# A graph network on one core: sum products ahead of query products, four index slots, node passes in four stages

## The chip, the cores and the metric

The kernel runs on one core of a Trainium2 chip. The metric is the device time of one execution in microseconds (us); lower is better. The engines of the core are TensorE (PE; its weight loads are listed as PEld), VectorE (DVE), ScalarE (ACT), GpSimd (POOL) and SyncE (SP), which issues most of the plain DMAs. Each engine runs its own stream of instructions in order, and the engines wait for each other on counting semaphores.

## The reference

Two graph layers over 6250 nodes with 128 features and 100,000 edges, sorted by destination. All data are float32.

```
x = norm(x + L0(x))          # attention layer
x = norm(x + L1(x))          # message layer

L0: q, k, v = X@Wq, X@Wk, X@Wv                     # 8 heads of 16
    scores  = sum(q[dst] * k[src]) / 4             # per edge and head
    alpha   = softmax of the scores over the edges of each dst
    agg     = segment_sum(alpha * v[src], dst)
    h1      = layer_norm(X + agg@W0)
    return layer_norm(h1 + relu(h1@fc1 + b)@fc2 + b)

L1: for the first and for the second half of the edges, with its own W1, W2:
        m = [x[src], edge_attr, req] ; h = relu(m@W1 + b1)@W2 + b2
        h_sum[dst] += h
    return relu(((1 + eps)*x + h_sum)@Wu + bu)
```

## The kernel before

After a short preparation (tables of chunks, key/value/query rows written to DRAM as kvq_tab) the kernel has three stages.

**First loop.** Edges are taken in chunks of 14 x 128 = 1792; there are 56. A chunk's edges end in a window of 128 nodes. GpSimd gathers the key and value rows of the edges' sources with one indirect DMA per 128 edges (L657), 14 a chunk, in four pieces of 4, 3, 4 and 3, into a ring of four chunk slots. TensorE spreads the window's queries over the edges (`queries`, L1050: 14 products of 128 x 128, each in two halves, so 28 instructions; four pieces). VectorE multiplies by the keys and reduces to scores, keeps the running maxima along the sorted edges by scans (`across`, L1404 to L1406, with help of TensorE's end transposes L1064/L1065 and carried transposes L1074/L1075), builds the one-hot masks (L1435) and weights the values (L1440) with the exponentials of ScalarE (L841 to L843). TensorE sums them into the window (L1090, 14 products, 28 instructions). A pass of the loop works on several chunks at once: the queries of the next chunk, the maxima of the last (`a_`), the sums of the one before (`b_`), the averages of the one before that (`c_`, L1080/L1081). In a pass TensorE's order is: end transposes, query pieces 0 and 1, carried transposes, averages' transpose, sums, query pieces 2 and 3.

The gathers are held by semaphores: piece 0 waits for the weighted values of the chunk four back (l_pvb), piece 1 for its sums (l_agg), piece 2 for the queries of the chunk one back (l_q), piece 3 for the end transposes of the chunk two back (l_lr).

**Node passes.** The 50 tiles of 125 nodes are taken in 10 groups of 5. A pass works on three groups: `new` (agg@W0, L1132, residual and first norm), `mid` (transposes, hidden layer L1115, relu L868, second product L1142) and `old` (second and third norm, transposes, then the products with W1 of both directions, L1152, copied by ScalarE, L906, and stored to y_tab by SyncE, L474). VectorE begins `old` at L1514. `passes3` writes two opening passes, a loop of 8 and two closing passes.

**Second loop.** 56 chunks again. GpSimd gathers rows of y_tab (L710), 14 DMAs a chunk, into a ring of four slots (yg). TensorE puts the attributes' share of the hidden layer into PSUM (L1187), VectorE adds it to the gathered rows (`hidden_rows`, L1575, semaphore m_hid), ScalarE takes the relu (L940), TensorE sums over the edges (L1200, semaphore m_agg), and finished windows go through Wu, the last norm and out. The indices (idx1), destination columns (dcol1) and attributes (eat) of a chunk are loaded by SyncE into two slots each. SyncE loads the attributes of chunk p+3 when the transposed attributes have been copied (m_eT), and the indices of chunk p+2 when VectorE has taken chunk p (m_hid). GpSimd's `gather_edges` waits for the indices (m_ix) and for the sums of the chunk four back (m_agg), and ahead of its second and third piece for the attribute transposes (m_eTp) and products (m_u).

Both loops are unrolled by four (`passes4`); every engine's counters advance by registers.

## Time and profile before

| | |
|---|---|
| median of 3 runs | 2862.45 us (2857.86 to 2866.96) |
| the profiled execution | 2882.01 us, span 2880.1 us |
| TensorE busy | 1588.5 us (55%), mean granted clock 0.711 |
| GpSimd busy | 1566.9 us (54%) |
| VectorE busy | 1430.9 us (50%) |
| ScalarE busy | 746.1 us (26%) |

The shares are averages over three stages. In a timeline row the number in brackets is the engine's idle time before the instruction and what ended it; "issue" means that it waited for nothing that the profile shows. In a row of windows each engine has its busy time and, behind x, the number of its instructions that began in the window; then come the granted TensorE clock (1.00 is 2.4 GHz, 0.50 is 1.2 GHz), the share of time in which the DMA engines were busy, and GB/s.

### The profile page before, as it was taken

The page shows a single profiled execution, that of the slowest core. Times are in us where ns is not written, and L with a number is a line of the kernel's source. Part 1 is how long each engine was busy: PE and PEld are TensorE (multiplying, and loading weights), DVE is VectorE, ACT ScalarE, POOL GpSimd, SP SyncE. Part 2 cuts the span into 40 slices and gives each one's busy share as a digit, 9 for nine tenths or more (in the row PEclk, how much of TensorE's full clock was granted, in tenths as well). Part 3 has the DMA queues.
Part 4 walks back from the last instruction along what each step waited for, and adds up shares of the span by engine and source line. Part 5 has one row for each costly group of instructions (what it writes and reads, how often), then busy time and mean ns, then how long its engine had stood idle before and what let it go on. Part 6 is the DMA issues. An engine that isn't in the chain of part 4 may idle for free.

```text
span 2880.1 us, 32266 instructions
## 1 busy us (share of the span) xinstructions
PE 1588.5 (55%) x7344; PEld 1255.8 (44%) x7345; DVE 1430.9 (50%) x2992; ACT 746.1 (26%) x1502; POOL 1566.9 (54%) x1648
## 2 busy tenths in 40 slices
PE   5315556565556565555777345555555555555546
PEld 3215555555555555554555233333433333333424
DVE  3226666666666666666555234343443333344435
ACT  2213333333333333333454111111111111111111
POOL 3346666666666666663111455655666665556653
PEclk8557676767776777776998667766676666666667
DMA  5474444444444444441000112211221121112211
GB/s 167 138 200 127 143 131 141 131 138 133 129 142 131 141 131 138 133 128 60 18 27 27 56 42 51 52 49 48 54 51 51 50 52 50 47 48 51 53 49 38
DMA packets 148162, 255.22 MB, mean 89 GB/s; under 512 B 73948, under 2 KB 99088, under 8 KB 147996
## 3 DMA queue, kind: packets, MB, share of 16 engines
q0 software_dynamic: 65072, 160.39, 19.9%
q1 hardware_dynamic: 81186, 92.67, 10.1%
q10 hardware_dynamic: 1870, 1.78, 0.2%
q8 instruction: 12, 0.20, 0.0%
q14 instruction: 22, 0.18, 0.0%
HBM read 233.05 MB, written 28.04 MB: 91 GB/s over the span
## 4 chain that ended last, share of the span: by engine, by line
issue 33%; PE 22%; DVE 16%; another core or an unknown queue 13%; DVEq 5%; DMA 5%; ACT 4%; SPq 1%; POOL 0%; ACTq 0%; POOLq 0%
PE ps L1090 8%; PE ps L1050 6%; DVE arena L1566 3%; DVE arena L1435 2%; DVE arena L1575 2%; PE ps L1200 2%; DVEq L1595 2%; PE ps L1187 1%; ACT arena L873 1%; PE ps L1152 1%; DVEq L1594 1%; DVE arena L1440 1%; DMA first<-d 1%; DVEq L1592 1%
## 5 line engine op out<-in xcount | busy, mean ns | idle before, releaser
L710 POOL DMA_INDIRECT arena<-y_tab,arena x784 | 741.9, 946 | 512.6 <-issue 494.1
L657 POOL DMA_INDIRECT arena<-kvq_tab,arena x784 | 749.0, 955 | 471.3 <-issue 240.6
L1050 PE MATMUL ps<-arena 128*128 128x128 f32 x1596 | 325.7, 363 | 331.0 <-issue 251.4
L1200 PEld LDWEIGHTS ps<-arena 128*128 128x128 f32 x1568 | 285.5, 247 | 413.2 <-issue 394.1
L1200 PE MATMUL ps<-arena 128*128 128x128 f32 x1568 | 308.0, 336 | 282.8 <-issue 273.5
L1050 PEld LDWEIGHTS ps<-arena 128*128 128x128 f32 x1596 | 299.5, 275 | 349.9 <-issue 345.5
L1090 PE MATMUL ps<-arena 128*128 128x136 f32 x1568 | 319.2, 391 | 173.3 <-DVE arena L1440 88.5
L1090 PEld LDWEIGHTS ps<-arena 128*128 128x128 f32 x1568 | 309.5, 295 | 190.6 <-issue 190.6
L940 ACT ACTIVATE arena<-arena 128x512 f32<-128x512 f32 x224 | 118.9, 567 | 1029.7 <-DVE arena L1575 662.7
L1575 DVE TENSOR_TENSOR arena<-ps,arena 128x512 f32<-128x512 f32 x224 | 127.8, 616 | 511.2 <-remote 299.1
L1187 PE MATMUL ps<-w1blk,eaT 113*128 x456 | 271.3, 677 | 59.4 <-issue 55.6
L809 ACT ACTIVATE arena<-arena 128x1792 f32<-128x1792 f32 x58 | 191.5, 3301 | 0.0
L1568 DVE TENSOR_REDUCE arena<-arena 128x128 f32<-128x1792 f32 x57 | 182.4, 3200 | 2.0
L1404 DVE COPY arena<-arena 8x1 f32<-8x1 f32 x56 | 7.9, 141 | 337.5 <-ACT arena L843 337.5
L832 ACT ACTIVATE arena<-ps 128x136 f32<-128x136 f32 x56 | 16.0, 285 | 507.4 <-remote 476.9
L1388 DVE TENSOR_REDUCE arena<-arena 128x32 f32<-128x512 f32 x224 | 139.2, 621 | 8.4 <-issue 0.5
L1386 DVE TENSOR_TENSOR arena<-ps,arena 128x512 f32<-128x512 f32 x224 | 135.9, 607 | 5.7 <-remote 3.0
L1187 PEld LDWEIGHTS ps<-w1blk,eaT 113*128 113x128 f32 x456 | 90.9, 240 | 75.1 <-issue 74.9
L1566 DVE TENSOR_TENSOR arena<-ps,arena 128x1792 f32<-128x1792 f32 x57 | 114.3, 2006 | 4.8 <-ACT arena L930 4.8
L1440 DVE TENSOR_TENSOR arena<-arena,ps 128x896 f32<-128x896 f32 x112 | 115.6, 1068 | 0.0
L1435 DVE TENSOR_TENSOR arena<-ps,arena 128x1792 f32<-128x1792 f32 x56 | 112.3, 2005 | 0.0
L1601 DVE TENSOR_TENSOR arena<-arena,ps 128x128 f32 x56 | 16.2, 288 | 190.2 <-issue 179.7
(243 smaller groups left out, 1980.5 us busy)
## 6 DMA issues: line engine op xcount, KB each, us to landing
arena<-d SPq DMA_DIRECT2D x58, 897.0 KB
arena<-kvq_tab,arena POOLq DMA_INDIRECT x784
arena<-y_tab,arena POOLq DMA_INDIRECT x784
eat<-ea SPq DMA_DIRECT2D x59, 112.0 KB
ea<-in_edge_attr_dram SPq DMA_DIRECT2D x2, 3125.0 KB, 20.0
y_tab<-arena SPq DMA_DIRECT2D x10, 625.0 KB
kvq_tab<-arena SPq DMA_DIRECT2D x6, 937.5 KB
arena<-kvq_tab SPq DMA_DIRECT2D x59, 64.0 KB
```

The lines of the kernel that those rows point to most:

```text
L657: g.indirect_dma_start(kv_s[:, r, t, :], None, kvq_tab.rearrange("n (a d) -> (n a) d", a=3), bass.IndirectOffsetOnAxis(ap=v3(idx, RING)[:, ...
L710: g.indirect_dma_start(yg_s[:, r, t, :], None, y_tab, bass.IndirectOffsetOnAxis(ap=v3(idx1, 2)[:, u, t:t + 1], axis=0)).then_inc(m_g[r][k] ...
L809: a.activation(hotT.rearrange("n (u g e) -> n u g e", u=2, g=G)[:, u, :, :], line.rearrange("n (e g) -> n g e", g=G), ACT.Relu, scale=-1.0 ...
L1050: last = mm(bank(k)[:, t * D:(t + 1) * D], hotT_s[:, u, s0 + t, :], v3(qwin, 2)[:, u, :])
L1090: last = mm(sums, hot_s[:, u, t, :], contrib_s[:, u, t * RW:(t + 1) * RW], start=(t == 0), stop=(t == G - 1))
L1187: mm(bank(j)[:, 0:n * D], eaT_s[:, u, k * P:(k + 1) * P], w1blk[:, ds(way + a0 * D, n * D)]).then_inc(m_u, 1)
L1200: last = mm(bank(6 + u)[:, 0:W], yg_s[:, r, t, :], hot1_s[:, u, t, :], start=(t == 0), stop=(t == G - 1))
L1435: tt(hot_s[:, u, :, :], columns[:, None, :].to_broadcast([P, G, P]), dcr_s[:, u, :, None].to_broadcast([P, G, P]), ALU.is_equal).then_inc( ...
L1440: tt(contrib_s[:, u, s0:s1, :, 0:DH], kv_s[:, r, s0:s1, D:2 * D].rearrange("p g (h w) -> p g h w", h=H), weights.rearrange("p (g h) -> p g ...
L1566: link(tt(hot1_s[:, u, :, :], columns1[:, None, :].to_broadcast([P, G, W]), dcr1[:, :, None].to_broadcast([P, G, W]), ALU.is_equal))
L1568: v.tensor_reduce(v3(hsum, 2)[:, u, :], hot1_s[:, u, :, :].rearrange("p g n -> p n g"), AX_X, ALU.add).then_inc(m_hot, 1)
L1575: tt(rows_, v3(bank(j)[:, 0:n * D], n), rows_, ALU.add).then_inc(m_hid, 1)
```

## The change

Three things are changed.

- First loop: in TensorE's pass the sum products (L1090) are placed ahead of the query pieces 0 and 1, the carried transposes and the averages' transpose. No other engine's order changes.
- Second loop: idx1, dcol1 and eat have four slots. SyncE loads all three for chunk p+4 in one place, after m_hid of chunk p; the first four chunks are loaded ahead of the node passes. GpSimd no longer waits for m_eTp and m_u. The attribute transposes still run three chunks ahead.
- Node passes: the last part of `old`, the products with W1 and their copy, becomes a fourth stage `out_` one pass later. These products go to banks 1 to 3, right behind the transposes of `mid`, and ScalarE copies them in two instructions ahead of the relus. ScalarE takes the square root of the second norm ahead of the relus, that of the third behind them, and finishes the third norm ahead of the first norm's root. VectorE computes the scales of the third norm ahead of the new group. TensorE puts the transposes of the third norm's result between the third and the fourth tile of the second hidden product. There are three opening passes, a loop of 7 and three closing passes. GpSimd's clearing of the accumulators moves behind the first group's sum.

```diff
@@ -221,8 +220,9 @@
         hsum = carve(2 * W)
         sel = carve(4)
-        idx1 = carve(2 * G).bitcast(I32)
-        dcol1 = carve(2 * G)
+        idx1 = carve(RING * G).bitcast(I32)
+        dcol1 = carve(RING * G)
+        eat = carve(RING * G * EA)
         dcr1 = carve(G)
         outT = carve(W)
...
@@ -467,6 +469,19 @@
             sp.wait_ge(l_qw[1], all_e)
             sp.sem_inc(l_over, 1)
+            sp.wait_ge(l_over, 4)
+            sp.wait_ge(s_eac, 32)
+            sp.wait_ge(s_tabi[1], 48)
+            eat_s = v3(eat, RING)
+
+            def load_chunk(chunk, r):
+                off = sp.value_load(tab_sb[1][0:1, ds(5 * chunk, 1)], min_val=0, max_val=NB * CH)
+                sp.dma_start(eat_s[:, r, :], ea1[ds(off, CH), :].rearrange("(p g) f -> p (g f)", g=G)).then_inc(m_at[r], 16)
+                sp.dma_start(v3(idx1, RING)[:, r, :], i1[ds(off, CH)].rearrange("(p g) -> p g", g=G)).then_inc(m_ix[r], 16)
+                sp.dma_start(v3(dcol1, RING)[:, r, :], d1[ds(off, CH)].rearrange("(p g) -> p g", g=G)).then_inc(m_ld[r], 16)
+
+            for c in range(RING):
+                load_chunk(c, c)
 
             sp.sem_inc(n_yfree, 2)
...
@@ -482,41 +497,19 @@
...
             def sp_msgs(r, new, a_, b_, c_):
                 u = r % 2
                 if new is not None:
-                    next_attr(new + 3, 1 - u)
                     sp.wait_ge(s_eac, 32)
                     sp.wait_ge(m_hid, spent)
-                    sp.wait_ge(m_dcr, prepared)
-                    load_edges(new + 2, u)
+                    load_chunk(new + RING, r)
                     sp.reg_add(spent, spent, NP_)
-                    sp.reg_add(prepared, prepared, 1)
+                    if r == RING - 1:
+                        sp.reg_add(loaded, loaded, 16)
                 if c_ is not None:
                     base = sp.value_load(tab_sb[1][0:1, ds(5 * c_ + 1, 1)], min_val=0, max_val=N - W)
...
@@ -691,41 +684,28 @@
 
             def gather_edges(r):
-                u = r % 2
                 pool.wait_ge(m_buf, 4)
-                pool.wait_ge(m_ix[u], landed)
+                pool.wait_ge(m_ix[r], landed)
                 pool.wait_ge(m_agg, slot_free)
                 for k, (s0, n) in enumerate(PIECES):
-                    if k in (1, 2):
-                        pool.wait_ge(m_buf, 4)
-                        pool.wait_ge(*((m_eTp, turned_) if k == 1 else (m_u, asked)))
                     for t in range(s0, s0 + n):
                         g.indirect_dma_start(yg_s[:, r, t, :], None, y_tab,
-                                             bass.IndirectOffsetOnAxis(ap=v3(idx1, 2)[:, u, t:t + 1], axis=0)).then_inc(m_g[r][k], 16)
+                                             bass.IndirectOffsetOnAxis(ap=v3(idx1, RING)[:, r, t:t + 1], axis=0)).then_inc(m_g[r][k], 16)
                 pool.reg_add(slot_free, slot_free, 1)
-                pool.reg_add(asked, asked, NP_)
-                pool.reg_add(turned_, turned_, 1)
 
             def gather_ring():
                 for r in range(RING):
-                    if r == 2:
-                        pool.reg_add(landed, landed, 16)
                     gather_edges(r)
                 pool.reg_add(landed, landed, 16)
...
             with pool.Fori(0, n1):
                 gather_ring()
-            pool.wait_ge(m_buf, 4)
-            pool.wait_ge(m_ix[0], landed)
-            pool.wait_ge(m_ix[1], landed)
             g.memset(mark[:, 1:2], 0.0)
 
...
@@ -873,37 +853,35 @@
                 return last
 
-            def act_pass(new, mid, old):
+            def act_pass(new, mid, old, out_):
                 if new is not None:
                     a.activation(v3(nTa, GRP), by_tile(new), ACT.Copy).then_inc(n_aT, 1)
...
                     act.wait_ge(n_hTp, mid + 1)
                     a.activation(nTh, bank(0, 2)[:, 0:GRP * P], ACT.Copy).then_inc(n_hT, 1)
-                    relu(mid, 0)
                 if old is not None:
                     sqrt(1, old, norm2)
+                if out_ is not None:
+                    act.wait_ge(n_y, out_ + 1)
+                    act.wait_ge(n_yfree, out_ + 1)
+                    y_ = yst[:, ds((out_ % 2) * (GRP * 2 * D), GRP * 2 * D)]
+                    a.activation(y_[:, 0:(GRP - 1) * 2 * D], bank(2, 2)[:, 0:(GRP - 1) * 2 * D], ACT.Copy)
+                    a.activation(y_[:, (GRP - 1) * 2 * D:GRP * 2 * D], bank(1)[:, D:3 * D], ACT.Copy).then_inc(n_ys, 1)
                 if mid is not None:
-                    relu(mid, 1)
-                if mid is not None:
-                    relu(mid, 2)
-                    relu(mid, 3)
+                    for c in range(FC):
+                        relu(mid, c)
                 if old is not None:
                     sqrt(2, old, norm2)
-                if new is not None:
-                    sqrt(0, new, norm1)
-                if old is not None:
                     act.wait_ge(n_r[1], old + 1)
                     normalised(v3(res2, GRP), v3(res2, GRP), norm2).then_inc(n_x1, 1)
                 if new is not None:
+                    sqrt(0, new, norm1)
                     act.wait_ge(n_r[0], new + 1)
                     normalised(v3(res, GRP), v3(res, GRP), norm1).then_inc(n_n1, 1)
...
                     act.wait_ge(n_x1c, old + 1)
                     a.activation(nTx, bank(0, 2)[:, 0:GRP * P], ACT.Copy).then_inc(n_xT, 1)
-                    act.wait_ge(n_y, old + 1)
-                    act.wait_ge(n_yfree, old + 1)
-                    a.activation(yst[:, ds((old % 2) * (GRP * 2 * D), GRP * 2 * D)], bank(4, 3)[:, 0:GRP * 2 * D], ACT.Copy).then_inc(n_ys, 1)
 
             act.sem_inc(n_ys, 1)
...
@@ -1063,6 +1039,16 @@
                     tp(left_right[0:H, 0:P], ends[:, :, G - 1], ident[:, :])
                     tp(left_right[0:H, P:2 * P], ends[:, :, 0], ident[:, :]).then_inc(l_lr, 1)
+                if b_ is not None:
+                    pe.wait_ge(l_hot, minus2)
+                    if c_ is not None:
+                        pe.wait_ge(l_cur, minus3)
+                    pe.wait_ge(l_pva, minus2)
+                    for t in range(G):
+                        if t == PVA:
+                            pe.wait_ge(l_pvb, minus2)
+                        last = mm(sums, hot_s[:, u, t, :], contrib_s[:, u, t * RW:(t + 1) * RW], start=(t == 0), stop=(t == G - 1))
+                    last.then_inc(l_agg, 1)
                 if new is not None:
                     queries(w, 0, True)
...
@@ -1115,42 +1091,56 @@
                 last.then_inc(n_f1, 1)
 
-            def pe_pass(new, mid, old):
+            def rows_y(t):
+                return bank(2, 2)[:, t * 2 * D:(t + 1) * 2 * D] if t < GRP - 1 else bank(1)[:, D:3 * D]
+
+            def pe_pass(new, mid, old, out_):
                 if mid is not None:
                     pe.wait_ge(n_h1, mid + 1)
+                    if out_ is not None:
+                        pe.wait_ge(n_xT, out_ + 1)
                     transposes(h1, n_hTp)
+                if old is not None:
+                    pe.wait_ge(n_z, old + 1)
+                if out_ is not None:
+                    pe.wait_ge(n_xT, out_ + 1)
+                    for t in range(GRP):
+                        if t == GRP - 1 and mid is not None:
+                            pe.wait_ge(n_hT, mid + 1)
+                        last = mm(rows_y(t), nTx[:, t * P:(t + 1) * P], w1x[:, :])
+                    last.then_inc(n_y, 1)
+                if mid is not None:
                     pe.wait_ge(n_hT, mid + 1)
-                    pe.wait_ge(n_ys, 1 if old is None else old + 1)
                     hidden(mid, 0)
                     hidden(mid, 1)
-                if mid is not None:
-                    pe.wait_ge(n_f1s, mid * FC + 1)
-                    hidden(mid, 2)
+                if out_ is not None:
+                    pe.wait_ge(n_ys, out_ + 2)
                 if new is not None:
                     pe.wait_ge(n_aT, new + 1)
...
                     last.then_inc(n_emb, 1)
                 if mid is not None:
-                    pe.wait_ge(n_f1s, mid * FC + 2)
-                    hidden(mid, 3)
-                    pe.wait_ge(n_f1s, mid * FC + FC)
-                    if old is not None:
-                        pe.wait_ge(n_v[1], old + 1)
+                    for c in range(2, FC):
+                        pe.wait_ge(n_f1s, mid * FC + (c - 1))
+                        hidden(mid, c)
                     for t in range(GRP):
+                        if t == GRP - 2 and old is not None:
+                            turn_rows(new, old)
                         for c in range(FC):
+                            if t == 0:
+                                pe.wait_ge(n_f1s, mid * FC + (c + 1))
                             last = mm(bank(2, 2)[:, t * D:(t + 1) * D], v3(ffT, FC)[:, c, t * P:(t + 1) * P], fc2_sb[:, c, :],
                                       start=(c == 0), stop=(c == FC - 1))
                     last.then_inc(n_f2, 1)
-                if old is not None:
-                    if new is not None:
-                        pe.wait_ge(n_v[0], new + 1)
-                    pe.wait_ge(n_x1, old + 1)
-                    transposes(res2, n_xTp)
-                    pe.wait_ge(n_xT, old + 1)
-                    for t in range(GRP):
-                        last = mm(bank(4, 3)[:, t * 2 * D:(t + 1) * 2 * D], nTx[:, t * P:(t + 1) * P], w1x[:, :])
-                    last.then_inc(n_y, 1)
+                elif old is not None:
+                    turn_rows(new, old)
+
+            def turn_rows(new, old):
+                if new is not None:
+                    pe.wait_ge(n_v[0], new + 1)
+                pe.wait_ge(n_x1, old + 1)
+                transposes(res2, n_xTp)
 
             pe.sem_inc(n_xTp, 1)
...
@@ -1511,7 +1500,8 @@
                     dve.wait_ge(n_xTp, old + 1)
                     hc3 = v3(h1c[:, ds((old % 2) * (GRP * D), GRP * D)], GRP)
-                    link(tt(q3, hc3, v3(bank(2, 2)[:, 0:GRP * D], GRP), ALU.add))
+                    tt(q3, hc3, v3(bank(2, 2)[:, 0:GRP * D], GRP), ALU.add).then_inc(n_z, 1)
+                    dve.wait_ge(n_z, old + 1)
                     statistics(q3, n_v[1], norm2)
                     dve.wait_ge(n_s[1], old + 1)
...
@@ -1519,15 +1509,13 @@
                     link(tt(q3, q3, xg(old), ALU.add))
                     statistics(q3, n_v[2], norm2)
+                    dve.wait_ge(n_s[2], old + 1)
+                    scales(norm2, n_r[1])
                 if new is not None:
 
...
                     link(tt(r3, xg(new), v3(bank(0, 2)[:, 0:GRP * D], GRP), ALU.add))
                     statistics(r3, n_v[0], norm1)
-                if old is not None:
-                    dve.wait_ge(n_s[2], old + 1)
-                    scales(norm2, n_r[1])
-                if new is not None:
                     dve.wait_ge(n_s[0], new + 1)
                     scales(norm1, n_r[0])
```

Left out of it: GpSimd's clearing of the accumulators, SyncE's three removed load functions for the second loop, the wider semaphore lists and counters, the passes with a fourth argument in `passes3`, the indices of slots in ScalarE's and TensorE's second loop, and the sums' old place (the ten lines shown as added after the end transposes are removed behind the averages' transpose).

## Rows read from the trace of the kernel before

**Rows 1.** Windows, all engines, by stage; columns: window, length, busy us (instructions) per engine, granted clock, DMA.
```profile
119.00:1355.00 1236.00, 702.58 (x3558) 638.61 (x3558) 768.42 (x1681) 425.76 (x733) 744.14 (x779) 0.71 0.45 136
1355.00:1607.00 252.00, 167.09 (x862) 125.23 (x862) 124.23 (x471) 118.17 (x213) 44.51 (x22) 0.85 0.07 26
1614.00:2880.00 1266.00, 667.88 (x2756) 461.49 (x2756) 506.17 (x730) 173.99 (x510) 742.04 (x785) 0.68 0.19 49
```

**Rows 2.** Timeline of a pass of the first loop: start, length, engine, line, operation, count [idle before, releaser].
```profile
623.87 0.95 POOL L657 DMA_INDIRECT arena<-kvq_tab,arena  x1 [3.69 <-remote]
...
624.90 2.66 PE L1050 MATMUL ps<-arena 128*128 128x128 f32 x14
...
625.95 0.14 DVE L1404 COPY arena<-arena 8x1 f32<-8x1 f32 x1 [6.66 <-ACT arena L843]
...
628.57 0.39 PE L1081 MATMUL ps<-arena 128*1 128x136 f32 x2
...
631.98 5.98 PE L1090 MATMUL ps<-arena 128*128 128x136 f32 x28 [3.02 <-DVE arena L1440]
...
637.79 0.67 PE L1050 MATMUL ps<-arena 128*128 128x128 f32 x4
...
641.66 0.69 SPq L365 DMA_DIRECT2D arena<-i  x1
...
643.82 2.06 PE L1050 MATMUL ps<-arena 128*128 128x128 f32 x8 [0.36 <-issue]
...
644.89 0.96 POOL L657 DMA_INDIRECT arena<-kvq_tab,arena  x1 [3.73 <-remote]
...
647.41 0.94 POOL L657 DMA_INDIRECT arena<-kvq_tab,arena  x1 [0.30 <-issue]
```

**Rows 3.** Windows of the same pass, before and during the gap at L1050.
```profile
623.87:638.50 14.63, 11.04 (x57) 10.02 (x56) 12.02 (x26) 7.21 (x12) 11.27 (x12) 0.66 0.54 164
638.50:643.80 5.30, 0.64 (x2) 0.47 (x2) 1.69 (x5) 0.00 (x0) 2.05 (x3) 0.69 0.29 82
```

**Rows 4.** Windows of the second loop, over one run of gathers.
```profile
2078.40:2089.10 10.70, 10.70 (x49) 7.43 (x49) 8.08 (x12) 2.78 (x9) 8.21 (x9) 0.72 0.27 66
2089.10:2117.00 27.90, 3.83 (x13) 2.04 (x12) 1.27 (x3) 1.44 (x4) 18.30 (x20) 0.60 0.21 54
```

**Rows 5.** Timeline of GpSimd (POOL) and SyncE (SP) in the second loop, restarts of the gathers.
```profile
1677.69 0.94 POOL L710 DMA_INDIRECT arena<-y_tab,arena  x1 [11.20 <-issue]
...
2056.17 0.95 POOL L710 DMA_INDIRECT arena<-y_tab,arena  x1 [9.09 <-issue]
...
2076.14 0.35 SPq L501 DMA_DIRECT2D arena<-i  x1
...
2078.45 0.95 POOL L710 DMA_INDIRECT arena<-y_tab,arena  x1 [5.06 <-issue]
...
2122.32 0.95 POOL L710 DMA_INDIRECT arena<-y_tab,arena  x1 [9.12 <-issue]
```

**Rows 6.** Timeline of a node pass.
```profile
1492.46 2.42 PE L1152 MATMUL ps<-w1x,arena 128*128 128x256 f32 x10 [1.68 <-ACT arena L903]
...
1493.47 0.82 DVE L1514 TENSOR_TENSOR arena<-arena,ps 128x640 f32<-128x640 f32 x1
...
1495.07 1.24 ACT L906 ACTIVATE arena<-ps 128x1280 f32 x1 [2.66 <-PE ps L1152]
...
1500.69 0.19 DVE L1492 RECIPROCAL arena<-arena 128x5 f32<-128x5 f32 x1 [4.67 <-ACT arena L864]
...
1514.93 0.82 DVE L1514 TENSOR_TENSOR arena<-arena,ps 128x640 f32<-128x640 f32 x1
```

**Rows 7.** Timeline of the start of the second loop.
```profile
1607.44 0.20 ACT L913 ACTIVATE mark<-eps_ln 128x1 f32<-128x1 f32 x1 [7.14 <-DMA y_tab<-arena]
...
1611.82 0.36 SPq L501 DMA_DIRECT2D arena<-i  x1
...
1614.21 0.99 POOL L710 DMA_INDIRECT arena<-y_tab,arena  x1 [18.46 <-DMA arena<-i]
```

More of the change, by code:

```diff
@@ L535, in _ @@
             sp.wait_ge(f_dma, stored)
+            for r in range(RING):
+                sp.wait_ge(s_eac, 32)
+                sp.wait_ge(m_at[r], loaded)
+                sp.wait_ge(m_ix[r], loaded)
+                sp.wait_ge(m_ld[r], loaded)
         @block.gpsimd
@@ L672, in _, with pool_pass @@
             pool.wait_ge(s_w4, 16 * (12 + 2 * (EG - 1)))
[L673 to L677 removed]
+            def pool_pass(new, mid, old, out_):
                 if new is not None:
@@ L1081, in pe_edges @@
                     mm(turned[0:1, W:W + RW], uc[:, w:w + 1], cur_s[:, w, :]).then_inc(l_ra, 1)
-                if b_ is not None:
-                    pe.wait_ge(l_hot, minus2)
-                    if c_ is not None:
-                        pe.wait_ge(l_cur, minus3)
-                    pe.wait_ge(l_pva, minus2)
-                    for t in range(G):
-                        if t == PVA:
-                            pe.wait_ge(l_pvb, minus2)
-                        last = mm(sums, hot_s[:, u, t, :], contrib_s[:, u, t * RW:(t + 1) * RW], start=(t == 0), stop=(t == G - 1))
-                    last.then_inc(l_agg, 1)
                 if new is not None:
@@ L1504, in _, with dve_pass @@
             rowb = lambda k: rows[:, k:k + 1, :].to_broadcast([P, GRP, D])
-            def dve_pass(new, mid, old):
+            def dve_pass(new, mid, old, out_):
                 xg = lambda at: v3(xs[:, ds(at * (GRP * D), GRP * D)], GRP)
```

84 lines of the change are left out of this document (29 added, 55 removed).

## The prediction

> **What bounds the kernel now.** I read the stages first, by windows. The first loop (the node features' attention, 56 chunks of 1792 edges) takes about 1236 us, the node passes 252 us, the second loop (the messages, 56 chunks again) 1266 us [rows 1]. In no stage is an engine busy all the time; GpSimd comes nearest in both loops, with one gather instruction of 0.95 us for 128 rows and 0.30 us between two [rows 2]. That is 14 x 1.25 = 17.5 us a chunk, 980 us for 56, against 21.0 us a chunk in the first loop (GpSimd starts again after its long wait at 623.87 and at 644.89, [rows 2]) and about 22.1 in the second (from the restart at 2056.17 to that at 2122.32 lie 66.2 us and three chunks, [rows 5]). So the question in both loops is what GpSimd and TensorE wait for beyond 17.5 us.
>
> The order of time in one pass of the first loop shows it [rows 2]. The 28 halves of the sum products run from 631.98 to 637.96. Four halves of the next chunk's third query product follow, and then TensorE nearly stands still: the next eight in a row begin only at 643.82. The window over that gap counts 2 matmuls in 5.30 us, against 57 in the 14.63 us before it [rows 3]. SyncE crawls in the same stretch (an index load takes 0.69 us to issue). GpSimd, whose next piece waits for the sums (l_agg), goes on only at 644.89, after 3.73 us of waiting. VectorE waits 6.66 us in such a pass (L1404), for the exponentials (L843), which wait for the end transposes (L1064) behind the queries in TensorE's order.
>
> The second loop shows the same thing more plainly. GpSimd starts a run of gathers at 2078.4, after a pause. For 10.7 us TensorE works normally: 49 matmuls. In the next 27.9 us it starts 13, while GpSimd issues 20 gathers; it recovers only when GpSimd has stopped [rows 4]. The pauses between runs are 5.06 and 9.12 us [rows 5]. I read this as one behaviour: after a stretch of uninterrupted gathers TensorE (and SyncE) get almost no instructions through, until GpSimd pauses and about 2.5 us have passed. In the first loop the stretch ends some 110 to 120 TensorE instructions after GpSimd's restart (57 matmuls and 56 weight loads in [rows 3]); in the second 49 and 49 plus its register instructions. GpSimd's pauses are then not only a loss: they are what lets TensorE move. The Trainium skill says otherwise: in "Runtime: NRT & Kernel Launch", "Instruction fetch mechanics", an engine's instruction buffer refills itself in the background and its cost is mostly hidden. By that page a run of gathers would cost TensorE nothing; the rows above show 13 matmuls in 27.9 us, and the rows decide.
>
> **Part 1, the sum products ahead of the queries.** Nothing is added or removed; the 28 halves of L1090 move ahead of the first two query products, the carried transposes and the averages' transpose. Those now stand between sums and the end transposes, which release VectorE's half of the pass. Before, they ran while VectorE worked on the masks, so they cost nothing. The cost from rows: 14 query halves 2.66 us, and about 1.2 us for the small products behind them (an estimate, three times the 0.39 us of L1081's pair), 3.9 us in all [rows 2]. Without any standstill the old cycle is sums 6.0, the third and fourth query products 1.6 to 3.0 (14 halves at 0.12 to 0.21 us), end transposes and exponentials about 1.5 (the last 1.05 lie between 624.90 and 625.95) and VectorE's part from L1404 to the start of the sums 6.0: 15.1 to 16.5 us. The new one is 19.0 to 20.4, above GpSimd's 17.5. Now the standstill. The old 21.0 is that cycle with 5.3 us of it. In the new order the sums begin about 12 to 14 us after the restart of GpSimd instead of 8 (from 623.87 to 631.98), so the standstill, which began 14.6 us after the restart, catches them half done; l_agg, for which GpSimd's next chunk waits, then comes after it. On the other side GpSimd's third piece waits for the queries (L653), now later than the sums, and may pause there 2 to 3 us while TensorE is working, which would spare part of the standstill. If the pause spares all of it, the pass takes 20.2 us (17.5 + 2.7): 0.8 us less than now. If it spares nothing, it takes up to 24.9 (21.0 + 3.9). A pass in between, one standstill for each restart at the queries, comes to about 22.3. I take that, as the chain really is longer: +1.3 us a chunk, 56 x 1.3 = **+73 us**, bounds -45 and +218.
>
> **Part 2, four slots for the indices.** It removes three kinds of wait of GpSimd: for the index load, for the attribute transposes (m_eTp) and for the attribute products (m_u); and one of SyncE's two stops a pass. Now a chunk's indices are loaded only when VectorE has taken the chunk two before (m_hid), by a SyncE that itself crawls. The restart at 2078.45 comes 2.3 us after such a load was issued, at 2076.14 [rows 5]. With four slots GpSimd is held only by m_agg of the chunk four back. The instructions saved (two loads of registers a pass) are on no path. If GpSimd were the bound, the loop would fall to 17.5 us a chunk: 4.6 x 56 = 258 us less. But the rows say that TensorE moves in the pauses. With the deeper slots GpSimd first runs 5 chunks in a row (88 us; now the first run, from 1614.21 on [rows 7], ends 52 us later, 11.20 us ahead of 1677.69 [rows 5]). Then it restarts when a sum is done. If TensorE finishes the next chunk (49 halves, 11 to 13 us at the rate of the first window of [rows 4]) before that run of 17.5 is over, the run doubles to 35 us and TensorE stands still for 24: a cycle of 47 to 49 us for two chunks, 24 a chunk, +106 us. If the standstill catches it just before the end of the sums, GpSimd pauses after each chunk, as in the first loop, 20.7 a chunk, -78 us. Today's runs of 28 and of 14 gathers alternate: 44 + 22 us for 3 chunks. I take no difference in the steady part, **0 us**, with those bounds.
>
> The loads before the node passes do gain a little. Now GpSimd starts at 1614.21, 6.8 us after the last store of the node passes has landed (1607.44), because the index load is issued at 1611.82 [rows 7]. With the indices in place it can start about 1608.5: **-6 us**.
>
> **Part 3, node passes in four stages.** A full pass takes 21.46 us (L1514 at 1493.47 and 1514.93) [rows 6]. The message products of a group (L1152, 2.42 us) and their copy (L906, 1.24 us) lie in its cycle between the norm and the next group's copies; they go a pass later, beside VectorE. VectorE's 4.67 us of waiting for a square root behind a relu (L1492) goes as well, since the root is put ahead. In exchange the second root waits behind all four relus, and the products stand ahead of the first hidden product. Adding up VectorE's own instructions with the three roots and one norm that it waits for gives 18.4 us, 3 less. That is 8 passes x 3.0 = **-24 us**; the pass more at the ends holds only the last product and copy, which the old last pass had too. Bounds: 8 x 4.67 = -37, and 0 if the new order only moves the wait. The memsets of GpSimd (L673, L674) move behind the first group's sum; they overlap TensorE and VectorE in both kernels.
>
> **The sum.** Against the profiled execution's own 2882.0 us (span 2880.1): +73 + 0 - 6 - 24 = +43, 2925. The median of the three runs shown, 2862.45, is 0.7% below it, so I forecast 2862 + 43 = **2905 us**.
>
> **Rivals.** (a) The standstill in the first loop stays where it is: the pause at the queries lets TensorE through, the pass remains at 21.0, and in the second loop GpSimd pauses after every chunk at 20.7. Then 0 - 78 - 30 = -108: 2754 us. For it: the old first loop does just that, at 21.0, every pass. Against it: the sums end nearer to the standstill by the 3.9 us moved ahead of them in time. It decides when the sums of a pass end within 14 us of GpSimd's restart. This is the one on the other side. (b) Only the node passes and the start count, the two loops keep their cycles: -30, 2832 us. The change of the loops would then do nothing; the near-equality of cycle and run length (17.3 us of gathers and 3.7 of pause in each pass) speaks for it. (c) Both loops lose: +73 or more, and the second loop in double runs at 24, +106, less 30: about 3010 us. (d) GpSimd really is the bound and both loops go to 17.5: 2862 - 196 - 258 - 30 = 2380; by the page on instruction fetch this would be the outcome for the second loop alone, 2862 - 258 - 30 = 2574. The windows of the second loop [rows 4] speak against both; I give them 0.03 together.
>
> **Chances.** Forecast 0.40; (a) 0.24; (b) 0.14; (c) 0.19; (d) 0.03. The range from 2750 to 3010 leaves out (d) and the outer parts of (a) and (c), 2 in 10. The forecast's own range is 2870 to 2950. A measurement of this kernel can tell 0.3% (9 us) from no change: faster 0.40, within it 0.06 (the rim of the forecast's range and of (b)), slower 0.54.
>
> **What would show it.** First loop: the distance of two GpSimd restarts (21.0 now), and where the gap of L1050 or L1090 sits; my step is wrong if no such gap is in the sums. If GpSimd pauses before piece 3 and the cycle is near 20, rival (a). Second loop: lengths of the runs of L710: only 14s mean 20.7, only 28s mean 24; a long first run of 70 gathers is expected in any case. TensorE's count of matmuls in a stretch of 28 gathers says whether it still stands still. Node passes: L1514 every 18.4 us, and L1492 without its 4.67 us. GpSimd's first L710 about 1.5 us after the last store has landed.

## The result: 2753.6 us, 0.9625 of the time before

| | before | changed |
|---|---|---|
| median | 2860.84 us (2857.86 to 2866.96, 4 runs) | 2753.56 us (2752.75 to 2757.68, 4 runs) |
| ratio | | 0.9625, 95% interval 0.9606 to 0.9644 |
| profiled execution | 2882.01 us | 2752.75 us, span 2750.9 us |

I had forecast 2905 us with a chance of 0.40 and, as rival (a), 2754 us with 0.24. The measured time is the rival's, to the microsecond. That closeness is luck: the experiments show that the rival was right for part of its reasons, and that its two terms were off in opposite directions.

One thing has to be said first, since every number below hangs on it. The experiments ran on eight chips, of two kinds. On two of them the kernel before took 2861.5 us and (in a single execution) 2896.1 us, near the result above: I call these slow chips. On six others its median was 2431 to 2435 us: fast chips. The prediction and the result are of a slow chip. Kernels are compared only with the kernel before on their own chip.

The windows of the changed kernel by stage (first loop, node passes, second loop), to be held against [rows 1]:

```profile
118.00:1348.00 1230.00, 626.36 (x3558) 569.04 (x3558) 770.05 (x1681) 428.04 (x735) 742.53 (x779) 0.71 0.45 137
1348.00:1544.00 196.00, 148.48 (x860) 116.06 (x860) 125.09 (x471) 118.69 (x221) 44.43 (x22) 0.92 0.09 32
1553.00:2750.00 1197.00, 684.78 (x2758) 473.13 (x2758) 507.39 (x731) 174.97 (x509) 740.32 (x785) 0.69 0.20 52
```

The first loop is 6 us shorter, the node passes 56, the second loop 69. Of this sum, more than the 107 us of the medians, some 20 are no effect of the change: the profiled execution of the kernel before lay 20 us above its median.

A pass of the first loop (timeline; compare [rows 2]):

```profile
635.79 0.94 POOL L649 DMA_INDIRECT arena<-kvq_tab,arena  x1 [3.35 <-remote]
...
646.18 6.51 PE L1050 MATMUL ps<-arena 128*128 128x136 f32 x28 [7.12 <-issue]
...
652.22 0.95 POOL L649 DMA_INDIRECT arena<-kvq_tab,arena  x1 [0.30 <-issue]
652.52 1.72 PE L1026 MATMUL ps<-arena 128*128 128x128 f32 x14
...
655.72 0.28 ACT L812 ACTIVATE arena<-ps 128x136 f32<-128x136 f32 x1 [6.67 <-remote]
...
656.48 0.94 POOL L649 DMA_INDIRECT arena<-kvq_tab,arena  x1 [3.31 <-remote]
```

L1050 is now the sum, L1026 the query product, L812 ScalarE's copy of the sums, which waits for l_agg as GpSimd does. The sums end at 652.69. The copy begins at 655.72, and GpSimd goes on at 656.48. So the signal of the sums was held for 3 us, and it came 2.55 us after GpSimd's last gather had ended (653.17). In the kernel before it was the same, and I had read it wrongly: the sums ended at 637.96, ScalarE's copy of them began at 644.13 and GpSimd's restart came at 644.89 [rows 2], and I put this down to the standstill of the *queries* behind them. A chunk takes 20.7 us now (635.79 to 656.48), 21.0 before.

GpSimd's restarts in the second loop (timeline; compare [rows 5]):

```profile
1982.14 0.94 POOL L697 DMA_INDIRECT arena<-y_tab,arena  x1 [3.70 <-remote]
...
2002.93 0.94 POOL L697 DMA_INDIRECT arena<-y_tab,arena  x1 [3.62 <-remote]
...
2023.47 0.94 POOL L697 DMA_INDIRECT arena<-y_tab,arena  x1 [3.30 <-remote]
...
2064.00 0.94 POOL L697 DMA_INDIRECT arena<-y_tab,arena  x1 [5.88 <-remote]
```

The pauses are 3.3 to 3.7 us after a run of 14 gathers, where they were 5.06, and 5.88 after one of 28, where they were 9.12. Both kinds of run now come to 20.3 to 20.8 us a chunk.

In a long run the signals do not wait for its end. These rows are from the run of 28 gathers that begins at 2023.47 and ends at 2058.11:

```profile
2032.60 0.30 PE L1211 MATMUL ps<-ident,arena 128*128 128x128 f32 x1 [2.30 <-DVE arena L1594]
...
2032.73 0.39 PE L1171 MATMUL ps<-ident,arena 128*112 128x128 f32 x2
...
2042.55 0.30 DVE L1577 BATCH_NORM_STATS2 arena<-ps 128x6 f32<-128x128 f32 x1 [7.97 <-issue]
...
2046.72 0.37 PE L1190 MATMUL ps<-arena 128*128 128x128 f32 x1 [2.21 <-issue]
...
2047.43 0.38 ACT L914 ACTIVATE eaT<-ps 112x256 f32<-112x256 f32 x1 [12.09 <-remote]
...
2049.52 0.37 PE L1190 MATMUL ps<-arena 128*128 128x128 f32 x1 [2.43 <-issue]
```

VectorE's L1577 waits for the product of L1211, ScalarE's L914 for those of L1171. Both were done 9.4 to 9.7 us into the run; their signals arrived 9.7 and 14.3 us later, in the middle of it. And TensorE itself is slow there: the halves of one piece of L1190, which have no wait between them in the program, start 2.8 us apart. So on this chip there are two effects while GpSimd gathers, late signals and a TensorE that hardly issues.

A node pass (DVE's L1503 is L1514 of before) is 17.15 us long, and here windows of whole passes say most. First seven passes of the kernel before, then two of the changed one, which are like the rest:

```profile
1401.46:1422.90 21.44, 14.16 (x86) 11.07 (x85) 12.39 (x49) 11.57 (x21) 2.85 (x2) 0.98 0.08 30
1422.90:1447.19 24.29, 17.27 (x86) 12.93 (x86) 12.38 (x48) 11.58 (x21) 2.83 (x2) 0.85 0.07 26
1447.19:1471.40 24.21, 18.72 (x90) 13.65 (x89) 12.39 (x49) 11.58 (x21) 2.83 (x2) 0.81 0.07 26
1471.40:1493.47 22.07, 15.80 (x88) 11.90 (x87) 12.37 (x48) 11.57 (x21) 2.84 (x2) 0.92 0.08 29
1493.47:1514.93 21.46, 14.20 (x86) 11.13 (x85) 12.38 (x49) 11.58 (x21) 2.83 (x2) 0.99 0.08 30
1514.93:1539.22 24.29, 17.34 (x86) 12.88 (x85) 12.38 (x49) 11.57 (x21) 2.83 (x2) 0.85 0.07 26
1539.22:1563.48 24.26, 18.80 (x90) 13.72 (x89) 12.37 (x48) 11.57 (x21) 2.84 (x2) 0.81 0.07 26
```

```profile
1389.96:1407.11 17.15, 14.00 (x86) 11.12 (x86) 12.49 (x48) 11.78 (x23) 2.84 (x2) 1.00 0.11 38
1407.11:1424.26 17.15, 14.00 (x86) 11.13 (x86) 12.50 (x48) 11.77 (x23) 2.83 (x2) 1.00 0.10 37
```

The pass that I costed, 21.46 us [rows 6], was one of the two quickest of seven; their mean is 23.15. In the others the granted clock was 0.81 to 0.92, part of the pass at the lower of the two levels, and TensorE's same work took 15.8 to 18.8 us instead of 14.2. In the new order the clock is 1.00 in all passes of this execution (in e11 below one of nine stretches has 0.91 and takes 1.7 us longer). From the first L1514 to the last the groups take 195.97 us before and 150.51 now. At the start of the second loop:

```profile
1551.04 0.20 ACT L891 ACTIVATE mark<-eps_ln 128x1 f32<-128x1 f32 x1 [7.12 <-DMA y_tab<-arena]
...
1553.01 0.98 POOL L697 DMA_INDIRECT arena<-y_tab,arena  x1 [13.70 <-PEq L299]
```

GpSimd starts 2.0 us after the last store, instead of 6.8 [rows 7].

### The profile page after: what moved, and what is told of

Its sections match the earlier page's. It is cut to its first block, busy times and chain, and to the rows that moved or that the text cites. A ratio compares the mean times of both kernels' runs of the same rounds, so it can differ in the third digit from the quotient of the medians.

```text
span 2750.9 us, 31824 instructions
## 1 busy us (share of the span) xinstructions
PE 1509.9 (55%) x7344; PEld 1188.5 (43%) x7345; DVE 1434.4 (52%) x2992; ACT 749.9 (27%) x1511; POOL 1563.0 (57%) x1647
## 4 chain that ended last, share of the span: by engine, by line
issue 27%; DVE 25%; PE 19%; another core or an unknown queue 16%; DVEq 5%; DMA 4%; ACT 2%; SPq 1%; POOL 1%; ACTq 0%; PEldq 0%; POOLq 0%
PE ps L1050 5%; PE ps L1026 4%; DVE arena L1424 4%; DVE arena L1554 3%; DVE arena L1375 3%; DVE arena L1429 3%; PE ps L1190 2%; PE ps L1177 2%; DVE arena L1563 2%; PE ps L1091 2%; DVEq L1583 1%; DVEq L1582 1%; DMA first<-d 1%; PE ps L1110 1%
## 5 line engine op out<-in xcount | busy, mean ns | idle before, releaser
L1050 PE MATMUL ps<-arena 128*128 128x136 f32 x1568 | 325.0, 396 | 418.8 <-issue 243.2
L1050 PEld LDWEIGHTS ps<-arena 128*128 128x128 f32 x1568 | 315.4, 300 | 437.8 <-issue 437.8
L1190 PEld LDWEIGHTS ps<-arena 128*128 128x128 f32 x1568 | 291.0, 252 | 377.4 <-issue 353.5
L1190 PE MATMUL ps<-arena 128*128 128x128 f32 x1568 | 316.0, 343 | 245.4 <-issue 237.8
L1177 PE MATMUL ps<-w1blk,eaT 113*128 x456 | 283.0, 703 | 65.2 <-issue 64.6
L1026 PE MATMUL ps<-arena 128*128 128x128 f32 x1596 | 243.9, 314 | 84.9 <-DVE arena L1375 52.1
L1026 PEld LDWEIGHTS ps<-arena 128*128 128x128 f32 x1596 | 225.6, 224 | 101.1 <-issue 101.1
L812 ACT ACTIVATE arena<-ps 128x136 f32<-128x136 f32 x56 | 15.9, 284 | 404.1 <-remote 371.5
L670 POOL TENSOR_TENSOR arena<-arena,rows 128x640 f32 (+1 forms) x10 | 15.4, 1540 | 181.6 <-DVE arena L1526 181.6
```

Of the source, the lines that this page charges most:

```text
L1026: last = mm(bank(k)[:, t * D:(t + 1) * D], hotT_s[:, u, s0 + t, :], v3(qwin, 2)[:, u, :])
L1050: last = mm(sums, hot_s[:, u, t, :], contrib_s[:, u, t * RW:(t + 1) * RW], start=(t == 0), stop=(t == G - 1))
L1177: mm(bank(j)[:, 0:n * D], eaT_s[:, u, k * P:(k + 1) * P], w1blk[:, ds(way + a0 * D, n * D)]).then_inc(m_u, 1)
L1190: last = mm(bank(6 + u)[:, 0:W], yg_s[:, r, t, :], hot1_s[:, u, t, :], start=(t == 0), stop=(t == G - 1))
```

## The experiments

**The parts one by one.** Each is the kernel before with one part of the diff of the change, and nothing else.

```diff
 e1_order:  the ten lines of the sums, moved as in the change
 e2_slots:  -idx1 = carve(2 * G) ... +idx1 = carve(RING * G), load_chunk, no m_eTp / m_u in gather_edges
 e3_nodes:  -def pe_pass(new, mid, old) ... +def pe_pass(new, mid, old, out_), the same on each engine
```

> The kernel before with the first loop's new order alone. My prediction's step would give +73 us (22.3 us a chunk). The reading of the profile after (TensorE's signals come free about 2.5 us after GpSimd stops gathering, whatever stands in TensorE's order) gives 20.7 us a chunk instead of 21.0: -17 us in the loop, some 10 given back behind it, so -10 us or so against before.

> The kernel before with the four index slots alone (and without the waits for m_eTp and m_u). My prediction: -6 us, steady part 0. If the late index load was what held each restart of the gathers, the second loop goes from 22.1 to 20.5 us a chunk: -87 us in the loop, about 19 given back at its end, -5 at its start: about -73 us.

> The kernel before with the four-stage node passes alone. My prediction: -24 us, bounds 0 and -37. The trace after shows passes of 17.15 us instead of 21.46: 8 x 4.3 = -34 us, with the opening and closing passes up to -48. The stages do not overlap the loops, so the three parts should add up to the whole change (-107 us).

All three met a fast chip (before 2434.8 us). The order gave 1.0021 (1.0006 to 1.0036), the slots 0.9995 (0.9981 to 1.0009), the node passes 0.9814 (0.9791 to 0.9838), which is -48 us by the medians. So on a fast chip the loops gain nothing (the order costs 5 us, barely clear of noise), and the node passes are worth twice my -24. The lengths of the node passes do not depend on the chip: the old ones take 21.4 to 24.3 us in the traces of e1 (fast) and e12 (slow) as well, the new ones 17.15 in that of e3.

**The whole change on a fast chip**, the kernel unaltered:

> The changed kernel, unaltered, on the chip of this call. In the first call the kernel before took 2434.8 us, not 2862: its trace of the loops shows GpSimd gathering without a pause (17.5 us a chunk in both loops), and the new order and the four slots changed nothing there. If the chip of this call is of that kind, the change is worth what the node passes are worth: 0.981, about 2387 us. If it is of the kind of the result (before at 2860), it is 0.9625 again.

It took 2387.8 us against 2435.4, 0.9812 (0.9791 to 0.9833): the node passes' gain and nothing more. The chain and the groups of its page show why:

```profile
POOL 35%; PE 21%; issue 15%; DVE 14%; DMA 10%; ACT 3%; SPq 1%; DVEq 1%; POOLq 0%; ACTq 0%; PEldq 0%
...
L649 POOL DMA_INDIRECT arena<-kvq_tab,arena x784 | 750.0, 957 | 291.1 <-issue 252.4
L697 POOL DMA_INDIRECT arena<-y_tab,arena x784 | 739.8, 944 | 252.3 <-issue 238.3
```

In the second loop GpSimd is busy 739.8 us and idle for 252.3, nearly all of it the 0.3 us between two gathers: 56 chunks of 17.5 us. After its first gather it never waits. And TensorE's signals are not late, though GpSimd gathers without a pause:

```profile
602.69 5.83 PE L1050 MATMUL ps<-arena 128*128 128x136 f32 x28 [6.87 <-DVE arena L1429]
...
608.56 0.28 ACT L812 ACTIVATE arena<-ps 128x136 f32<-128x136 f32 x1 [3.01 <-PE ps L1050]
```

The copy begins 0.04 us after the sums have ended. The same groups of the changed kernel on the slow chip:

```profile
L649 POOL DMA_INDIRECT arena<-kvq_tab,arena x784 | 747.4, 953 | 458.0 <-issue 247.2
L697 POOL DMA_INDIRECT arena<-y_tab,arena x784 | 740.2, 944 | 422.8 <-issue 228.5
```

A gather costs the same. What a slow chip adds is 166.9 and 170.5 us of waiting in the two loops, the pauses of 3.4 us and more.

**The slots on a slow chip.**

```diff
 e12_slots: the kernel of e2_slots
```

> The kernel before with the four index slots alone, on the chip of this call. Slow chip: the restart of the gathers no longer waits for an index load behind the recovery, 20.5 us a chunk in the second loop instead of 22.1, about -70 us against before. My prediction's step says -6. Fast chip: 0.9995 again.

2812.3 us against 2861.5 on the same chip: 0.9819 (0.9771 to 0.9867), -49 us, less than the -70 expected. From the first to the last gather of the second loop it takes 1155.9 us, against 1235.1 in the profiled execution before; but behind the last gather 55.0 us are left, against 30.8. The shorter pauses are worth 79 us, and 24 of them are given back behind the last gather. Its first loop, in the old order, shows these restarts:

```profile
501.94 0.94 POOL L647 DMA_INDIRECT arena<-kvq_tab,arena  x1 [3.44 <-remote]
...
522.63 0.94 POOL L647 DMA_INDIRECT arena<-kvq_tab,arena  x1 [3.37 <-remote]
...
543.35 0.94 POOL L647 DMA_INDIRECT arena<-kvq_tab,arena  x1 [3.36 <-remote]
```

That is 20.7 us a chunk with the old order too. The 21.0 of [rows 2] belong to an execution that lay 20 us above its median; the new order as such has given no gain that I can show on either kind of chip. -49 for the slots (slow chip) and -48 for the node passes (fast chip, with passes of the same length) are 97 of the 107 us; the 10 left lie within the interval of the former (14 us to either side).

**The change with the old order kept.**

```diff
 e17_old_order: after, with
-                if b_ is not None:        (the ten lines of the sums)
                 if new is not None:
                     queries(w, 0, True)
...
+                if b_ is not None:        (back behind the averages)
```

> The changed kernel with the first loop's old order (four slots and four-stage node passes kept). Fast chip: the new order alone measured 1.0021 against before, so this is 0.979, some 5 us below the changed kernel's 0.981. Slow chip: if the new order is worth the 0.3 us a chunk that the two first traces show, 2765 us; if that was the difference of one profiled execution from the median, 2753 as the changed kernel, ratio 0.9625.

2382.0 us against 2434.5, 0.9785 (0.9763 to 0.9807), on a fast chip: the intervals of this and of the changed kernel (0.9791 to 0.9833) overlap, though with e1's 1.0021 they point the same way, to a new order that costs some 5 us. It is the lowest ratio of a complete kernel on a fast chip. On a slow chip it was not run.

**The chain without the gathers.** Both kernels gather only the first 128 edges of each piece, 4 of 14; the other rows are zeros.

```diff
-                    for t in range(s0, s0 + n):
+                    for t in range(s0, s0 + 1):
                         g.indirect_dma_start(kv_s[:, r, t, :], None, ...
```

> The kernel before with 4 gathers a chunk instead of 14 in both loops (the first of each piece; the other rows are zeros, filled once by two memsets of GpSimd, some 12 and 6 us), so that GpSimd is no bound and hardly ever busy: what remains is the chain over TensorE, VectorE and ScalarE. My prediction gives 15.1 to 16.5 us a chunk in the first loop with the old order, and 12 to 15 in the second. If the gathers are what holds up TensorE on a slow chip, its matmuls follow each other here without gaps of 2 us on any chip.

> The changed kernel with the same 4 gathers a chunk. My prediction gives 19.0 to 20.4 us a chunk in the first loop with the new order, 3.9 more than the old one. Against it: on two chips the first loop took 17.65 us a chunk in both orders, so the new chain cannot be above 17.5; then it is some 16 to 17 us, or the new order costs the chain nothing. Second loop as with the old kernel, 12 to 15.

These met a slow chip (before 2896.1 us), with one execution each: 1928.1 us with the old kernel and 2012.4 with the new. GpSimd's waits for the sums, old kernel first:

```profile
503.06 0.95 POOL L659 DMA_INDIRECT arena<-kvq_tab,arena  x1 [3.31 <-PE ps L1094]
...
518.87 1.05 POOL L659 DMA_INDIRECT arena<-kvq_tab,arena  x1 [4.52 <-PE ps L1094]
...
533.21 0.98 POOL L659 DMA_INDIRECT arena<-kvq_tab,arena  x1 [3.63 <-PE ps L1094]
...
547.44 0.95 POOL L659 DMA_INDIRECT arena<-kvq_tab,arena  x1 [3.15 <-PE ps L1094]
```

```profile
499.79 0.94 POOL L651 DMA_INDIRECT arena<-kvq_tab,arena  x1 [3.64 <-PE ps L1054]
...
516.86 0.95 POOL L651 DMA_INDIRECT arena<-kvq_tab,arena  x1 [3.88 <-PE ps L1054]
...
534.35 0.94 POOL L651 DMA_INDIRECT arena<-kvq_tab,arena  x1 [4.28 <-issue]
...
551.02 0.94 POOL L651 DMA_INDIRECT arena<-kvq_tab,arena  x1 [3.85 <-PE ps L1054]
```

Three chunks take 44.4 us in the old order, 14.8 each, and 51.2 in the new, 17.1 each. So the new order does lengthen the chain of TensorE and VectorE, by 2.3 us (I had said 3.9), but to 17.1: still under the 17.5 us of the gathers. It matters only where the gathers are few. And with few gathers the sums' signal is not held on a slow chip: in seven of these eight waits the releaser is named and is the sum's own line, and ScalarE's copy begins 0.03 us (old) and 0.04 us (new) after the sums have ended.

**Is it TensorE's own number of instructions?** Six of the 14 sum products of each chunk are left out, in both loops.

```diff
+                        if t % 2 and t != G - 1:
+                            continue
                         last = mm(sums, hot_s[:, u, t, :], ...
```

> The changed kernel without 6 of the 14 sum products of each chunk in both loops (the sums are of fewer edges). On a chip where the gathers hold up TensorE: if TensorE runs dry after some 115 of its own instructions, 24 fewer a chunk let it finish a chunk's sums before that, GpSimd is held later or not at all, and the time falls below 2700 us; if what counts is the time that GpSimd has gathered without a pause (about 14 us), nothing changes: 2750 us. On a chip where they do not, GpSimd is the bound at 17.5 us a chunk and nothing changes beside the changed kernel, under 5 us.

> As the half-sums kernel before, on the chip of this call. Slow chip (before near 2860 to 2900): if TensorE runs dry after some 115 of its own instructions in a run of gathers, it is held later in time than with all sums and at the same count; if the length of GpSimd's run counts, it is held at the same time (about 14 us into the run) and at a lower count, some 90 to 95. Fast chip: 2385 us, nothing new.

e6 met a fast chip, 2384.2 us, and so did a repetition (e10_half_sums, 2379.5 us against 2431.6): as the changed kernel. e11 met a slow chip: 2734.5 us against 2861.5, 0.9547 (0.951 to 0.9585), some 20 us below what the change's 0.9625 would be there (the changed kernel itself was not run on that chip). A run of gathers in its first loop, windows and timeline:

```profile
622.70:635.50 12.80, 3.44 (x16) 3.37 (x16) 12.23 (x28) 7.18 (x12) 9.76 (x11) 0.56 0.54 170
```

```profile
622.67 0.95 POOL L649 DMA_INDIRECT arena<-kvq_tab,arena  x1 [3.32 <-remote]
...
632.16 3.97 PE L1052 MATMUL ps<-arena 128*128 128x136 f32 x16 [9.36 <-DVE arena L1433]
...
639.00 0.95 POOL L649 DMA_INDIRECT arena<-kvq_tab,arena  x1 [0.30 <-issue]
...
642.47 0.28 ACT L812 ACTIVATE arena<-ps 128x136 f32<-128x136 f32 x1 [7.45 <-remote]
...
643.23 0.95 POOL L649 DMA_INDIRECT arena<-kvq_tab,arena  x1 [3.27 <-remote]
```

TensorE has started 16 matmuls in the first 12.8 us of the run, where it had 57 in 14.63 in [rows 3]. The sums end 13.5 us after the restart, at 636.13, and their signal is held for 6.3 us, again until 2.5 us after the last gather (639.95). Of TensorE's instructions it is far from the 110 to 120 that I had read as the condition. TensorE does not stand still at that point either: it starts seven query products at 635.92, and its own first gap comes only at 640.6, after 46 matmuls and 44 weight loads since the restart. So a count of 110 to 120 is the condition for neither. In three programs the sums were done 14.1, 16.9 and 13.5 us into a run of 14 gathers, and each time their signal arrived 2.5 to 3.0 us after the last gather of the run had ended. For a run of 14 the signal follows GpSimd's run, not TensorE's work. Where in a run the holding begins is not shown, and in the run of 28 above signals come late but before its end.

**Does the rate of the gathers matter, or the length of the run?** Four kernels were to tell, all built on the changed one.

```diff
 e4_slower_gathers, behind each gather:
+                        for _n in range(6):
+                            pool.reg_mov(idle_, BASE)
 e9_mid_pause (4), e13_short_pause (2), behind the seventh gather of a chunk:
+                    for _n in range(4 if k in (1,) else 0):
+                        g.memset(idle[:, :], 0.0).then_inc(e_idle, 1)
+                        pool.wait_ge(e_idle, idled)
+                        pool.reg_add(idled, idled, 1)
 e14_piece_stops: the same once, 16 columns wide, behind each piece
```

> [...] Where TensorE is held up while GpSimd gathers: if a backlog behind GpSimd is the cause, slower gathers let it drain and the pauses of 3.4 us vanish, so the time falls by about 50 to 100 us; if not, the pauses stay and it rises by up to 280 us.

> The changed kernel in which GpSimd waits in the middle of each chunk's gathers (behind the seventh) for four chained memsets of 128x400, some 1.8 us, in both loops. On a fast chip (before at 2435) it adds 1.8 us to each chunk of both loops, about 200 us, to 2590. On a slow chip (before at 2860 to 2900): if a short pause lets TensorE catch up, its signals are not held at the end of a chunk, the pause of 3.4 us there vanishes, and a chunk takes 19.3 us instead of 20.7: 2600 us. If only a pause of 2.5 us or more helps, the 1.8 us come on top: 22.5 us a chunk, 2950 us.

> The changed kernel with a pause of GpSimd of some 1.35 us (two chained memsets; four took 2.7 us) behind the seventh gather of each chunk in both loops. Fast chip: 1.35 us on each of 112 chunks, 2387 + 150 = 2540. Slow chip: if what holds TensorE's signals is a backlog that grows with an unbroken run of gathers (17.3 us now), two runs of 9 us do not reach it, the pause of 3.4 us at the chunk's end goes, and a chunk takes 18.9 us: 2550. If a pause must be longer than 1.35 us to help, 22 us a chunk: 2890.

> The changed kernel with a very short stop of GpSimd (one memset of 128x16 and the wait for it, some 0.4 us) behind each of the four pieces. Fast chip: 1.6 us a chunk, 2570. Slow chip: if the mean rate of the gathers is what counts, the backlog does not build and a chunk takes 19 us: 2580. If only the length of a pause counts, the stops come on top of the 20.7 us: up to 2930.

All ran on fast chips: 2384.7, 2676.8, 2558.9 and 2709.0 us, ratios 0.9798 (0.9766 to 0.9829), 1.1001 (1.0963 to 1.1039), 1.0527 (1.0486 to 1.0569) and 1.1145 (1.1112 to 1.1177). The two pauses ran three times more (e15_short_pause, e16_mid_pause, e18_short_pause), on fast chips again, 2559.6, 2678.8 and 2561.2 us. They say one thing. On a fast chip every microsecond that GpSimd loses in a chunk comes out in the time: (2676.8 - 2387.8) / 112 = 2.6 us a chunk for a pause of 2.7, 1.5 for 1.35; GpSimd is the bound there, fully. The register moves, for which I had reckoned with up to 280 us, cost nothing (2384.7 us): the gathers start 1.26 us apart on average with and without them, so this kernel says nothing of their rate. The short stops cost 2.9 us a chunk, 0.7 each instead of the 0.4 that I had taken. What the pauses would do on a slow chip stays open.

## Why the prediction was wrong, step by step

- **What bounds the kernel.** Right that the loops stand between GpSimd's 17.5 us and a standstill while it gathers: on fast chips, where there is no standstill, they take 17.5. Wrong in the condition ("110 to 120 instructions") and in taking it for a standstill of TensorE alone: e11 has the sums' signal held when TensorE had started 16 matmuls and was still at work. In "Runtime: NRT & Kernel Launch", "Instruction fetch mechanics", the Trainium skill says that the cost of fetch is mostly hidden. On fast chips, at 17.5 us a chunk, the trace agrees: TensorE is idle for 34.2 us in all ahead of the matmuls of L1190, against 245.4 on the slow chip. On slow chips I had set the rows against the page; for the late signals they are no evidence against it, and whether fetch has a part in TensorE's own standstill (2.8 us between two halves of L1190 above) no run tells.
- **Part 1, +73 us: the step that failed.** I took it that the new order would push the sums into the standstill, so that l_agg, for which GpSimd waits, would come later. But its signal arrived after the standstill in the old order already. GpSimd's period is 17.4 us of gathers, some 2.5 us until the held signal is there, and 0.8 to restart, 20.7 in all, with the sums done 14.1 us or 16.9 us into the run alike. Measured: 1.0021 on a fast chip (5 us), 20.7 us a chunk in both orders on a slow chip. The longer chain is real (17.1 against 14.8 us; I had said 19.0 to 20.4 against 15.1 to 16.5), and hidden even at 17.5. The pause at the queries that I reckoned with never came: GpSimd stops once in 14 gathers, at the sums.
- **Part 2, 0 us with bounds -78 and +106.** Measured -49 us on a slow chip (e12). I had the row for it: the load at 2076.14, the restart 2.3 us later [rows 5]. Every long pause of the old second loop stands ahead of the first gather of a chunk (after 42, 70, 84, 112 gathers and so on), where GpSimd waits for m_ix and m_agg; the waits for m_eTp and m_u held nothing. I read it so: the index load was last in a chain that starts when TensorE's signals come free (not tested apart from the other parts of the slots). With m_agg alone in its place, the pause falls by 1.5 us after a run of 14 and by 3.2 after one of 28. I had set it against double runs at 24 us a chunk. They come, but at (2064.00 - 2023.47) / 2 = 20.3. The first run, which I expected to be 70 gathers long, is 56: four chunks, as many as the ring has slots. On a fast chip the part is worth nothing. The start of the second loop gave -4.8 of the -6.
- **Part 3, -24 us.** The mechanism held, the size was off by two: -48 us alone (e3). The terms that I undersized: the old pass, 21.46 instead of a mean of 23.15 (the granted clock in five of seven), and the new one, 17.15 instead of 18.4. Over the seven passes between them that is 42 us, and the shorter first and last stretch make it 45.5 (195.97 to 150.51).
- **Rival (a)**, 2754 us: its parts were -78 for the second loop and -30 for the rest; measured -49 and -48, so its total came out by two errors that cancel. Its first loop, unchanged by the new order, was right. The reason that it gave for this, the pause at the queries, and its condition (sums done within 14 us of the restart) were wrong: they end at 16.9. **Rival (d)**, 17.5 us a chunk in both loops, is what fast chips do, in both kernels, so there too it is no gain of the change.
- Open are what makes a chip slow, whether rate or length of a run of gathers is the condition, how TensorE's late signals and its slow issue belong together, and whether a pause in mid-run helps there.

## What to carry to other kernels

Before you cost a move in an engine's order, look at when the signal of the moved work reaches the engine that waits for it; if it is already held by something later than the work itself, the move is free, both ways. Take the length of a repeated pass from all its passes, with the granted clock of each, not from the one that you read in detail. A bound that rests on waits with the releaser "remote" or "issue" may belong to the chip and not to the kernel: run both kernels on more than one chip before you build on it.

## What the hardware showed that was not expected

- One program takes 2431 to 2435 us on six chips and 2861 to 2896 on two; a gather takes the same 0.95 us on both. On a slow chip signals of TensorE are late while GpSimd gathers: in runs of 14 gathers the sums' signal came 3.0 to 6.3 us late, 2.5 to 3.0 us after the run had ended; in a run of 28 two signals came 9.7 and 14.3 us late, before its end. With 4 gathers a chunk the sums' signal is not late.
- The page of a slow chip has no landing time for the gathers, that of a fast chip has. The DMA issues of the changed kernel, slow chip, then fast:

```profile
arena<-kvq_tab,arena POOLq DMA_INDIRECT x784
arena<-y_tab,arena POOLq DMA_INDIRECT x784
```

```profile
arena<-kvq_tab,arena POOLq DMA_INDIRECT x784, 2.8
arena<-y_tab,arena POOLq DMA_INDIRECT x784, 2.5
```

Landings are missing from the record on both slow chips and in the result's two profiles, also with 4 gathers a chunk, where the signal is not late. All executions here were recorded, so it can't be said whether the recording has a part in it.

- Six register moves of GpSimd behind each gather cost no time (2384.7 us against 2387.8); a memset of 128x16 with the wait for it costs 0.7 us.
